# A block of attention between two routed feed-forward layers: rope components in tiles of their own, one instruction for the normalised output, one product for the causal mask

## The reference, cut to what matters

```python
qkv = x @ Wqkv.T                               # b=32, t=512, 3*256
q, k, v = jnp.split(qkv, 3, axis=-1)           # 16 heads of 16
q = cos * q + rotate_half(q) * sin             # rotate_half: (-x[1::2], x[::2]) interleaved
k = cos * k + rotate_half(k) * sin
scores = jnp.einsum('bhqd,bhkd->bhqk', q, k) / math.sqrt(DH)
scores = jnp.where(causal, scores, -jnp.inf)
attn = jax.nn.softmax(scores, axis=-1)
out = jnp.einsum('bhqk,bhkd->bhqd', attn, v)
```

## Time and profile before

| | |
|---|---|
| runs, median (lowest to highest) | 2402.93 us (2398.98 to 2409.86) |
| profiled execution | 2401.97 us |
| its span | 2400.2 us |
| TensorE busy | 2190.0 us, 91% |
| VectorE busy | 1956.3 us, 82% |
| ScalarE busy | 1357.7 us, 57% |
| GpSimd busy | 1280.2 us, 53% |

### The profile page before, as it was taken

One profiled execution on the slowest core, in us unless ns is written; L12 is line 12 of the kernel. 1 busy time (PEld: TensorE's weight loads), 2 busy tenths in 40 slices (PEclk: granted clock), 3 DMA queues, 4 the chain that ended last, 5 costly groups with the idle time before them and its releaser, 6 DMA issues. The chain is left out here.

```text
span 2400.2 us, 56572 instructions
## 1 busy us (share of the span) xinstructions
PE 2190.0 (91%) x19596; PEld 1279.8 (53%) x19596; DVE 1956.3 (82%) x4345; ACT 1357.7 (57%) x2567; POOL 1280.2 (53%) x1458
## 2 busy tenths in 40 slices
PE   2999999399999999999999999999999986999999
PEld 1666666245554555555455455545545543666666
DVE  4777777379989989998998999899899864777776
ACT  2455545046666666666666666666666663455454
POOL 3666666335545544554554555455455424666664
PEclk9999999779999999999999999999999997999999
DMA  5566665323444444344344434444433513665664
GB/s 162 172 203 204 203 204 191 88 63 89 97 89 93 95 92 90 89 99 89 93 95 89 90 90 99 89 96 94 86 90 92 93 39 111 187 210 193 208 205 164
DMA packets 280284, 295.50 MB, mean 123 GB/s; under 512 B 45664, under 2 KB 263104, under 8 KB 280000
## 3 DMA queue, kind: packets, MB, share of 16 engines
q1 hardware_dynamic: 279456, 290.83, 46.8%
q10 hardware_dynamic: 544, 1.05, 0.1%
HBM read 140.08 MB, written 83.89 MB: 93 GB/s over the span
## 5 line engine op out<-in xcount | busy, mean ns | idle before, releaser
L817 ACT ACTIVATE at_probs<-at_st_ps 128x512 f32<-128x512 f32 x1280 | 748.2, 604 | 508.6 <-PE at_st_ps L924 499.1
L750 DVE TENSOR_REDUCE at_mx<-at_mx_ps 128x1 f32<-128x512 f32 (+3 forms) x1408 | 839.8, 634 | 141.3 <-PE at_mx_ps L905 139.6
L672 POOL TENSOR_SCALAR_AFFINE_SELECT at_probs<-at_probs 128x512 f32<-128x512 f32 x512 | 320.5, 639 | 710.6 <-ACT at_probs L817 710.6
L899 PE MATMUL at_mx_ps<-at_k_stack,at_q_stack 48*128 48x512 f16 (+3 forms) x2048 | 502.3, 303 | 20.7 <-DVE at_mx L750 10.7
L924 PE MATMUL at_st_ps<-at_q_stack,at_k_stack 49*128 49x512 f16 (+3 forms) x2048 | 459.5, 302 | 65.7 <-ACT at_probs L817 64.2
L428 ACT ACTIVATE f_h<-f_h_ps,f_b1s 128x512 f32<-128x512 f32 x256 | 176.0, 688 | 359.2 <-PE f_h_ps L470 347.7
L924 PEld LDWEIGHTS at_st_ps<-at_q_stack,at_k_stack 49*128 49x128 f16 x2048 | 135.8, 94 | 433.4 <-ACT at_probs L817 332.0
L904 PE MATMUL at_mx_ps<-mask,turn 64*128 64x128 bf16 (+2 forms) x1408 | 342.2, 243 | 0.0
L941 PE MATMUL at_pv_ps<-at_probs,at_v 128*32 128x512 f32 (+3 forms) x4096 | 331.4, 441 | 0.3 <-POOL at_probs L672 0.3
L905 PE MATMUL at_mx_ps<-mask,turn 64*128 64x64 bf16 (+2 forms) x1408 | 281.5, 200 | 0.0
L486 PE MATMUL f_y_ps<-f_w2hi,f_hlo 128*128 128x256 f16 x1024 | 279.1, 273 | 0.0
(11 more groups left out here) (118 smaller groups left out, 4240.0 us busy)
## 6 DMA issues: line engine op xcount, KB each, us to landing
at_q_stack<-qk_image SPq DMA_DIRECT2D x192, 128.0 KB, 4.3
at_k_stack<-qk_image SPq DMA_DIRECT2D x192, 128.0 KB, 4.4
f_x<-in_x SPq DMA_DIRECT2D x32, 512.0 KB, 5.6
f_w1hi<-w_hi SPq DMA_DIRECT2D x128, 128.0 KB, 2.3
f_w1lo<-w_lo SPq DMA_DIRECT2D x128, 128.0 KB, 2.1
f_b2s<-in_b SPq DMA_DIRECT2D x128, 128.0 KB, 3.7
f_w2hi<-w_hi SPq DMA_DIRECT2D x128, 128.0 KB, 4.2
f_w2lo<-w_lo SPq DMA_DIRECT2D x128, 128.0 KB, 4.2
```

What stands on the lines that cost most here:

```text
L672: nc.gpsimd.affine_select(out=ap, in_=ap, compare_op=ALU.is_ge, fill=0.0, base=0, pattern=[[0, d] for d in dims] + [[1, P]], channel_multi ...
L750: nc.vector.tensor_reduce(o_ap, i_ap, AX_X, ALU.max).then_inc(max_done, 1)
L817: nc.scalar.activation(probs[:, c, :], st_ps[c % 2][:], ACT.Exp, scale=DH ** -0.5).then_inc(exp_done, 1)
L899: nc.tensor.matmul(bank[:, at * w:at * w + w], q_stack[s.par][rows, j + a, i * P:(i + 1) * P], k_stack[s.par][rows, j + a, 0:w], start=(at ...
```

## The change

Rope: the host orders the columns of the q and k weights so that tile 0 of q holds the even components of all heads and tile 1 the odd ones, at the same partitions (k: tiles 2 and 3). ScalarE copies each projected tile to `raw`, after VectorE has multiplied it by cos, at steps 3 and 7 of slots 0 and 1. GpSimd multiplies `raw` by sin tile by tile, but makes both rotated tiles behind the odd one: even = cos part of even minus sin part of odd, odd = cos part of odd plus sin part of even. The images in HBM are read with another pattern of rows.

Output: one product of 256 elements in place of four of 64.

Mask: constants of 64 rows whose one product is hugely negative above the diagonal and negligible elsewhere, so that L905 falls away.

```diff
@@ gpsimd, rope @@
                 pool.wait_ge(rope_in, idx + 1)
-                nc.gpsimd.tensor_tensor(by_sin[t % 2][:], swapped[t % 2][:], sin_t[:], ALU.mult).then_inc(sin_done, 1)
-
-                wait(pool, qk_lo, idx - 1)
+                nc.gpsimd.tensor_tensor(by_sin[t % 2][:], raw[t % 2][:], sin_t[:], ALU.mult).then_inc(sin_done, 1)
+                if t % 2 == 0:
+                    return
+
                 pool.wait_ge(sin_done, idx + 1)
-                nc.gpsimd.tensor_tensor(rotated[t % 2][:], by_cos[t % 2][:], by_sin[t % 2][:], ALU.add).then_inc(rope_done, 1)
+                for e, op in ((0, ALU.subtract), (1, ALU.add)):
+
+                    wait(pool, qk_lo, idx - 2 + e)
+                    nc.gpsimd.tensor_tensor(rotated[e][:], by_cos[e][:], by_sin[1 - e][:], op).then_inc(rope_done, 1)
@@ vector, begin_rope @@
-                nc.vector.tensor_tensor(by_cos[t % 2][:], x_ps[t % 2][:], cos_t[:], ALU.mult)
-                nc.vector.stream_shuffle(swapped[t % 2][:], x_ps[t % 2][:], [i ^ 1 for i in range(32)]).then_inc(rope_in, 1)
+                nc.vector.tensor_tensor(by_cos[t % 2][:], x_ps[t % 2][:], cos_t[:], ALU.mult).then_inc(cos_done, 1)
@@ vector, normalise_output @@
-                for i in range(NT):
-                    ins = nc.vector.tensor_tensor(
-                        on[os.par][:, i, :].rearrange("p (j q d) -> p j q d", q=2, d=DH)[:, j:j + GH, half, :],
-                        turned[:, i, :, 0:DH],
-                        inverse[:, GH * i:GH * i + GH].rearrange("p (a d) -> p a d", d=1).broadcast_to([P, GH, DH]), ALU.mult)
-                ins.then_inc(on_done, 1)
+                nc.vector.tensor_tensor(
+                    on[os.par][:].rearrange("p i (j q d) -> p i j q d", q=2, d=DH)[:, :, j:j + GH, half, :],
+                    turned[:, :, :, 0:DH],
+                    inverse[:].rearrange("p (i a d) -> p i a d", i=NT, d=1).broadcast_to([P, NT, GH, DH]), ALU.mult).then_inc(on_done, 1)
@@ scalar @@
+            def rope_raw(n, t):
+                idx = 4 * n.b + t
+                act.wait_ge(cos_done, idx + 1)
+
+                wait(act, sin_done, idx - 1)
+                nc.scalar.activation(raw[t % 2][:], x_ps[t % 2][:], ACT.Copy).then_inc(rope_in, 1)
...
                     if g in (1, 2) and sample(s + 1) and n in (0, 2):
                         rope_high(s + 1, 2 * (g - 1) + (n == 2))
+                    if g < 2 and sample(s + 1) and n in (3, 7):
+                        rope_raw(s + 1, 2 * g + (n == 7))
@@ tensor, max_scores @@
-                nc.tensor.matmul(last, tab.turn[const, HP:3 * HP], over.broadcast_to([HP, nh, P]), start=False, stop=False)
-                nc.tensor.matmul(last[:, :, HP:P], tab.turn[const, 0:P], over[:, :, 0:HP].broadcast_to([HP, nh, HP]),
-                                 start=False, stop=True).then_inc(mx_done, 1)
+                nc.tensor.matmul(last, tab.turn[const, :], over.broadcast_to([HP, nh, P]), start=False, stop=True).then_inc(mx_done, 1)
@@ sync, read_stack @@
-                        img = image[2 * part + lo].rearrange("(j a r) n -> a r j n", a=2, r=DH)[par]
+                        img = image[2 * part + lo].rearrange("(r j a) n -> a r j n", a=2, r=DH)[par]
@@ host @@
+    halves = np.arange(D).reshape(H, DH // 2, 2).transpose(2, 1, 0).reshape(-1)
+    columns = np.concatenate([halves, D + halves, 2 * D + np.arange(D)])
-        "WqkvT": np.asarray(L0_attn_Wqkv).T,
+        "WqkvT": np.asarray(L0_attn_Wqkv).T[:, columns],
```

More of the change, by code:

```diff
@@ L135, in _ @@
             sp.dma_start(tab.b1[:], b1T).then_inc(loaded["b1"], 16)
-            sp.wait_ge(half_masked, 1)
+            sp.wait_ge(half_masked, 2)
+            sp.dma_start(tab.turn[HP:P, :], tab.turn[0:HP, :]).then_inc(loaded["b1"], 16)
             sp.dma_start(tab.mask[HP:P, :], tab.mask[0:HP, :]).then_inc(loaded["b1"], 16)
-            sp.wait_ge(loaded["b1"], 32)
+            sp.wait_ge(loaded["b1"], 48)
         @block.scalar
@@ L161, in _ @@
             nc.vector.tensor_tensor(tab.wo.lo[:], wof[:], tab.wo.hi[:], ALU.subtract).then_inc(tables_done, 1)
-            dve.wait_ge(tables_done, 8)
+            dve.wait_ge(tables_done, 7)
         @block.gpsimd
@@ L169, in _ @@
             nc.gpsimd.memset(tab.turn[:], 0.0).then_inc(ident_zeroed, 1)
-            nc.gpsimd.memset(tab.mask[:], -1e30).then_inc(ident_zeroed, 1)
+            nc.gpsimd.memset(tab.mask[:], 0.0).then_inc(ident_zeroed, 1)
             pool.wait_ge(ident_zeroed, 3)
@@ L174, in _ @@
                                     base=0, pattern=[[-1, P]], channel_multiplier=1).then_inc(tables_done, 1)
[L176 to L183, removed]
+            q_of, k_of = tab.turn[0:HP, :], tab.mask[0:HP, :]
+            nc.gpsimd.affine_select(out=q_of, in_=q_of, compare_op=ALU.is_ge, fill=2.0 ** 64,
+                                    base=0, pattern=[[1, P]], channel_multiplier=-2).then_inc(ident_zeroed, 1)
+            nc.gpsimd.affine_select(out=k_of, in_=k_of, compare_op=ALU.not_equal, fill=-2.0 ** -24,
+                                    base=0, pattern=[[1, P]], channel_multiplier=-2).then_inc(ident_zeroed, 1)
+            pool.wait_ge(ident_zeroed, 5)
+            nc.gpsimd.affine_select(out=q_of, in_=q_of, compare_op=ALU.not_equal, fill=2.0 ** -20,
+                                    base=0, pattern=[[1, P]], channel_multiplier=-2).then_inc(half_masked, 1)
+            nc.gpsimd.affine_select(out=k_of, in_=k_of, compare_op=ALU.not_equal, fill=-2.0 ** 60,
+                                    base=-1, pattern=[[1, P]], channel_multiplier=-2).then_inc(half_masked, 1)
 def ffn_phase(nc, tag, tab, src, dst, Wr, br, b2):
@@ L525, in attention_phase @@
         xT = Split(sb("xThi", [P, NC, T], F16), sb("xTlo", [P, NC, T], F16))
-        swapped = [sb(f"swapped{i}", [P, T], F32) for i in range(2)]
+        raw = [sb(f"raw{i}", [P, T], F32) for i in range(2)]
         by_cos = [sb(f"by_cos{i}", [P, T], F32) for i in range(2)]
@@ L554, in attention_phase @@
         xT_lo, qk_done, rope_in, sin_done = sem("xT_lo"), sem("qk_done"), sem("rope_in"), sem("sin_done")
+        cos_done = sem("cos_done")
         rope_done, qk_hi, qk_lo, v_done = sem("rope_done"), sem("qk_hi"), sem("qk_lo"), sem("v_done")
@@ L1063, in program @@
         tab.ident = sb("ident", [P, P], F32)
-        tab.turn = sb("turn", [P, 3 * HP], BF16)
+        tab.turn = sb("turn", [P, P], BF16)
         tab.mask = sb("mask", [P, P], BF16)
@@ L1085 @@
     freqs = np.exp(np.float32(-np.log(10000.0)) * np.arange(0, DH, 2, dtype=np.float32) / np.float32(DH)).astype(np.float32)
-    angles = np.arange(T, dtype=np.float32)[None, :] * freqs[(np.arange(P) % DH) // 2][:, None]
-    sign = np.where(np.arange(P) % 2 == 0, -1.0, 1.0).astype(np.float32)[:, None]
+    angles = np.arange(T, dtype=np.float32)[None, :] * freqs[np.arange(P) // H][:, None]
+    halves = np.arange(D).reshape(H, DH // 2, 2).transpose(2, 1, 0).reshape(-1)
+    columns = np.concatenate([halves, D + halves, 2 * D + np.arange(D)])
     ins = {
         "x": L0_attn_x,
-        "WqkvT": np.asarray(L0_attn_Wqkv).T,
+        "WqkvT": np.asarray(L0_attn_Wqkv).T[:, columns],
         "WoT": np.asarray(L0_attn_Wo).T,
@@ L1098 @@
         "cos": np.cos(angles).astype(np.float32),
-        "sin": (np.sin(angles) * sign).astype(np.float32),
+        "sin": np.sin(angles).astype(np.float32),
     }
```

## The result

The changed kernel takes 2606.18 us (median of four runs, 2604.59 to 2612.71) against 2404.89 us (four runs, 2398.98 to 2409.86): a ratio of 1.0843, 95% interval [1.0811, 1.0875]. Forecast were 2503 us and a range of 2440 to 2545. The direction was right, the size was not: 201 us instead of 101.

What follows compares the result with a forecast made beforehand. TensorE and VectorE, both near full and tied step by step, were taken to bound the kernel. Slot 2's 4.3 us delay less 0.25, 0.4 and 0.4 saved, over 31 samples, adds 101 us: 2503 us, range 2440 to 2545.

Steps and rivals of the forecast that it cites:

- Part 4, the chain: Late rotation delays `rope_low` and maximum 1 on VectorE; TensorE's step 3 in slot 1 starts 1.75 us late.
- Parts 1 and 2: TensorE saves a counted 0.4 us a slot on mask products; VectorE saves 3.3 us a sample on shuffles and output.
- The rival by which a product is worth 0.12 us: On TensorE, each dropped 64-column mask product saves 0.12 us: 169 us in place of 50, total 2384 us; chance 0.12.
- The prediction's other estimate, 114 us: On TensorE, 1408 dropped mask pairs at about 81 ns would give back 114 us in place of 60.
- Part 3, the copy: ScalarE's four copies a sample to `raw`, 0.59 us each; ScalarE has room, only the second copy's wait counted.
- The sum: Delays less savings over the four slots: 3.25 us longer a sample, 101 us over 31 samples.
- The snowball rival: Late exponentials and blocked port hit both slots, rotations take 1.54 us: 4.7 us a sample, 2548 us; chance 0.12.

Runs made afterwards that it cites:

- e1: Changed kernel with rotated tiles taken up later, by ScalarE at steps 2 and 4 and VectorE at steps 3 and 4: 2433.37 us.
- e3: Kernel before with the rope change alone, keeping the old mask and output: 2632.44 us, ratio 1.0931.
- e5: Changed kernel with only VectorE taking up the rotated tiles later, ScalarE still at step 0: 2444.65 us.
- e6: Kernel before with the one mask product alone: 2376.38 us, ratio 0.9889.
- e2: Kernel before with the new mask and the single output instruction, old rope kept: 2364.59 us, ratio 0.9845.
- e9: Changed kernel with ScalarE's raw copy put behind its copy of pv_ps in step 3: 2629.35 us, ratio 1.0945.
- e4: Changed kernel with six matmuls of zeros added in step 2 of slots 1 and 2 to keep TensorE busy: 2543.10 us.
- e12: Changed kernel with six matmuls of zeros added in slot 2 only: 2546.50 us, ratio 1.0598.
- e10: Changed kernel with the layer norm statistics of slot 2 at step 3 instead of 1: 2545.32 us, ratio 1.0593.
- e11: Changed kernel with six matmuls of zeros added in slot 1 only: 2632.47 us, ratio 1.0963.

## Why the prediction was wrong in size

*Part 4, the chain: right.* Forecast 5.7 and 8.5 us from mask 3, measured 5.65 and 8.46, with the blocked `rope_low` in it. e1, e3 and e5 show that this is the cause, and that VectorE's place in it decides. Slot 2 at full clock was to be 2.95 us longer and is 2.94.

*Parts 1 and 2: right as far as they were timed.* e6 and e2 give 27 and 39 us; slots 2 and 3 save 0.25 and 0.31 us against 0.25 and 0.4 forecast. No run times the loss of the shuffles by itself. The rival by which a product is worth 0.12 us is refuted: it gave 169 us, and e6 measured 27. The prediction's other estimate, 114 us, was worked out from the figure of the Trainium skill ("TensorE: Matmul & The Clock Gate", Back-to-back issue gap) for 128 columns. e6's 27 us for 1408 products doesn't bear it out here, where most of them had 64 columns and all were of half height.

*Part 3, the copy: the first step that failed.* I priced ScalarE's copy at nothing at step 3, "ScalarE has room", and looked only at its second place. It stands ahead of the copy for which TensorE waits at step 5. Slot 0 was to save 0.4 us and saved none; slot 1 was to be 1.1 us longer, and is 1.65 at full clock. e9 gives both back, 0.43 and 0.57 us. Together they make the 4.3 us a sample at full clock out of 3.25: 31 x 1.0 = 31 us.

*The clock: the step that is missing.* The sum took the earlier trace rows's granted clock of 1.00 as given, and did not ask what becomes of it when the sum itself makes two slots of each sample late by one to three microseconds each. e4 prices it at 63 us; no rival had it. 2503 + 31 + 63 = 2597 us, against 2606; most of the 9 us left are the six slots in which e4's clock still falls, each over a microsecond longer than at full clock. The Trainium skill ("TensorE: Matmul & The Clock Gate", HAM oscillation — how this bites in real kernels) says that waits inside a loop can send the clock down in every turn and be paid for again in the next matmuls. The trace agrees that it comes again and again: 0.50 from 1047 to 1055 us, and so in slot 2 of 20 samples. But the page's case is an engine that stands still while it waits for a DMA, and here TensorE was busy 1.47 of the 3 us before the clock fell. The prediction drew on that page for the mask product alone.

The snowball rival (2548 us) came near to the 2543 of e4, but that is luck, since its mechanism isn't there: rotations took 1.27 us each, not 1.54.

## What to carry to other kernels

A step that is moved back is priced by who takes it up: here the take-up of the even tile, one instruction on ScalarE and one on VectorE, stayed at step 0 while its input moved from early in the previous slot to behind its end, and taking both tiles up later gave 173 us back. The engine that waits longest isn't always the one that costs: what stands queued behind the wait decides, so walk each queue, also for a copy "with room to spare". And where TensorE runs at its full clock in a tight loop, a stall has a second price; if the granted clock of the changed kernel is under that of the one before, part the two with work that keeps TensorE busy and adds nothing.

## What the runs showed of the hardware that was not expected

- 384 matmuls of zeros more make the kernel 63 us faster (e4), or 60 us with half of them, all in slot 2 (e12).
- The half clock is not decided by the busy share of the stall alone: before 981.2 and before 1033 us TensorE was busy 1.51 of 3 us with the same instructions at the same distances, and the clock fell to 0.50 the first time and stayed at 1.00 the second. Which samples are hit, and for how long, changes with small shifts (e9, e10, e11), and what picks them is open.
- A tiny VectorE instruction with two inputs in SBUF (128 by 4) takes 1.25 us in place of 0.16 beside GpSimd's addition, and ends with it, at 1030.14 against 1030.11 us. `rope_low` was held back by it too, 1.08 us against 0.69. This is e1, the second statistics instruction, and GpSimd's subtraction and addition (1027.61 to 1030.11):

```profile
1028.81 0.17 DVE L103 TENSOR_TENSOR at_pair<-at_stats 128x4 f32<-128x4 f32 x1
1028.89 1.25 DVE L104 TENSOR_TENSOR at_pair<-at_stats 128x4 f32<-128x4 f32 x1
...
1027.61 2.50 POOL L691 TENSOR_TENSOR at_rotated<-at_by_cos,at_by_sin 128x512 f32<-128x512 f32 x2
```
